# Moving q's stores and loads from SyncE's queue to GpSimd's, and splitting the first key segment ahead of q

## The chip, the cores and the metric

The kernel runs on one core of a Trainium2 chip. The metric is the time of one execution on the device in microseconds; the median of several executions is given. The trace is that of one profiled execution, whose times count from the start of its span.

## The reference

The program is one transformer layer with cross attention and a mixture of experts. What matters here is the attention in front:

```python
q = (layernorm(x) @ Wq + bq)        # x: 1024 x 128, 16 heads of 8
k = (ctx @ Wk + bk)                 # ctx: 6404 x 96
v = (ctx @ Wv + bv)
attn = softmax(clip(einsum('bhqd,bhkd->bhqk', q, k) * 8 ** -0.5, -1e4, 1e4))
x = x + einsum('bhqk,bhkd->bqhd', attn, v).reshape(1, 1024, 128) @ Wo + bo
x = x + ffn(layernorm(x))           # a main FFN and the best two of eight experts, gelu
```

All of it is computed in float32.

## The kernel before

**Stages.** First come the projections. TensorE transposes the context in 13 chunks of 512 keys (`ctx_transpose`), ScalarE copies each chunk to SBUF (`evac_ctxT`), TensorE projects it to keys (`project_k`) and ScalarE copies the result to `kT` (`evac_k`, semaphore `k_ready`). Between chunks 3 and 4 TensorE transposes the normalised x (`xnT`) and projects q, which ScalarE writes as `qT` (`q_ready`). VectorE does the layer norm ahead of that, copies `xnT` out of PSUM, and takes the largest absolute value of each chunk of `kT` (`range_k`), from which a bound on the scores is formed.

**Parts and round trips.** Scores are made with four-byte numbers of a rounded kind, so q and k are each split into a rounded part and the rest (`split_q`, `split_k`: one cast and one subtraction each). The parts go to DRAM and come back in another layout, in which the parts of the eight dimensions of one head stand on 32 partitions. For k this goes by ten segments of 640 keys: `split_k(s)` writes `kparts[:, s % 2]` (two buffers, so segment s waits until the store of segment s - 2 has landed), `store_k` stores it with two DMAs, `load_k` loads it to its place in `region_k`. For q it is once for all: `split_q` writes `qparts`, two stores go to `q_dram`, and then `load_q` loads each of four head groups with four DMAs of 32 partitions x 4 KB (each row of DRAM goes to two partitions) to `qst`. `qparts` lies in the first 2048 columns of `region_k`, in which the first key segments are to land later.

**Order.** All of these DMAs are on SyncE's queue (SP): the context and x, the two q stores, a wait for them, the loads of q's group 0, then the key segments' stores and loads in turn, then the loads of q's groups 1 to 3. GpSimd (POOL) makes constants, sets the row of ones in `region_ctxT` (after the last `xn`), sets the ones of `v9` and issues ten weight loads for later stages.

**Attention.** `score_tile(0)` waits for q's group 0 and key segment 0. Behind it on TensorE stand the projections of the first two chunks of v. Then follow 500 tiles of 3 x 512 scores: TensorE makes the scores (L1094), ScalarE the exponentials (L521), TensorE the products with v (L1179). Some score blocks go to VectorE instead, by a plan that is written out (`D_PLAN`) and starts at tile 37. The other v chunks, and the bounds, are spare jobs between the first tiles, and the splits of key segments 4 to 9 stand behind such v jobs. Segment s is first read some 6.7 s tiles into a pass (20 score blocks for each segment, three to a tile). All orders are fixed in the program: no engine chooses.

Of the kernel before, what the change touches and what calls it, by code (L numbers as in the profile page):

```python
# [22 lines left out]
NQ, C, CK, NK = 1024, 128, 96, 6404  # L23
# [10 lines left out]
BANK = 512  # L34
# [153 lines left out]
def build(nc, x, ctx, wq, bq, wk, bk, wv, bv, wo, bo, alpha, w_gate, b_gate, w1m, b1m, w2m, b2m,  # L188
# [4 lines left out]
    with ExitStack() as stack:  # L193
# [53 lines left out]
        q_abs = xn_flat  # L247
        att_tok = xn
        attT = xnT
        qparts = region_k[:, 0:PARTS * NQ].bitcast(F32R).rearrange("p (a n) -> p a n", a=PARTS)  # L250
        vtail = sb("vtail", [P, NG, P])
        qst = sb("qst", [P, NG, NQ], F32R)
        hid = [region[:, 0:CB * NQ].rearrange("p (c n) -> p c n", c=CB) for region in (region_kT[:, 2 * BANK:], region_ctxT)]
# [121 lines left out]
        def evac_k(act, c):  # L375
            a, b = c * BANK, min((c + 1) * BANK, NK)
            act.wait_ge(k_psum, c + 1)
            act.activation(kT[:, a:b], bank(3 + c % 3, P, b - a), ACT.Copy,
                           accum_out=ksum[:, c:c + 1]).then_inc(k_ready, 1)
# [8 lines left out]
        @block.sync  # L388
        def _(sp):

            rows = ctx[0, 0:FULL * P, :].rearrange("(p t) c -> p t c", t=FULL)
            for i, (t0, t1) in enumerate(zip(CTX_AT[:-1], CTX_AT[1:])):
                sp.dma_start(ctx_sb[:, t0:t1, :], rows[:, t0:t1, :]).then_inc(ctx_in[i], 16)
                if i == 0:
                    sp.dma_start(xres[:, :, :], x[0].rearrange("(t p) c -> p t c", p=P)).then_inc(x_in, 16)
            sp.dma_start(ctx_tail[:, :], ctx[0, FULL * P:NK, :]).then_inc(tail_in, 16)

            for b in range(PARTS):
                sp.wait_ge(qparts_ready, b + 1)
                sp.dma_start(q_dram[:, :, b, :], qparts[:, b, :].bitcast(F32)).then_inc(qparts_stored, 16)  # L400
            sp.wait_ge(qparts_stored, 16 * PARTS)
            load_q(sp, 0)
            for s in range(NSEG):
                store_k(sp, s)
                if s != 1:
                    load_k(sp, 0, max(s - 1, 0))
            load_k(sp, 0, NSEG - 1)
            load_k_tail(sp)
            for g in range(1, NG):
                load_q(sp, g)  # L410
            sp.wait_ge(flag_ready, 1)
            safe = sp.value_load(flag[0:1, 0:1], min_val=0, max_val=1)
            with sp.If(safe != 0):
                for g in range(1, NG):
                    for s in range(NSEG):
                        sp.wait_ge(scores_ready, tile_of_segment(NHALF * g - 1, s) + 1)
                        if spare_of_segment(g - 1, s):
                            sp.wait_ge(spare_psum, spare_of_segment(g - 1, s))
                        load_k(sp, g, s)
            with sp.Else():  # L420
                for s in range(NSEG):
                    sp.wait_ge(kst_in[s], 16)
                for g in range(NG):
                    sp.wait_ge(qst_in[g], 16 * GH)
                sp.wait_ge(ktail_in, 16 * NG)

            sp.wait_ge(topk_ready, 1)
            load_expert(sp, 0)
            for n, (t0, t1) in enumerate(OUT_TILES):
                sp.wait_ge(res_ready, n + 1)  # L430
                sp.dma_start(out[0, t0 * P:t1 * P, :].rearrange("(t p) c -> p t c", p=P), xn[:, t0:t1, :]).then_inc(out_stored, 16)
            sp.wait_ge(out_stored, 16 * len(OUT_TILES))


        @block.gpsimd
        def _(pool):
            pool.memset(ident[:, :], 0.0).then_inc(const_zero, 1)
            pool.memset(ones[:, :], 1.0).then_inc(const_ready, 1)
            pool.memset(hmask[:, :], 1.0).then_inc(const_zero, 1)
            pool.wait_ge(const_zero, 1)  # L440
            pool.affine_select(out=ident[:, :], in_=ident[:, :], compare_op=ALU.not_equal, fill=1.0, base=0,
                               pattern=[[-1, P]], channel_multiplier=1).then_inc(const_ready, 1)
            pool.wait_ge(const_zero, 2)

            pool.affine_select(out=hmask[:, :], in_=hmask[:, :], compare_op=ALU.is_ge, fill=0.0, base=0,
                               pattern=[[-D, H]], channel_multiplier=1).then_inc(const_zero, 1)
            pool.wait_ge(const_zero, 3)
            pool.affine_select(out=hmask[:, :], in_=hmask[:, :], compare_op=ALU.is_ge, fill=0.0, base=D - 1,
                               pattern=[[D, H]], channel_multiplier=-1).then_inc(const_ready, 1)
            pool.wait_ge(const_ready, 3)  # L450
            for dst, src in ((wv_sb[0:CK, :], wv), (wv_sb[CK:CK + 1, :], bv)):
                pool.dma_start(dst, src).then_inc(wv_in, 16)
            pool.memset(tailT[:, :], 0.0).then_inc(pads_ready, 1)
            pool.wait_ge(pads_ready, 1)
            pool.memset(ktail[:, :, :].bitcast(F32), 0.0).then_inc(pads_ready, 1)
            pool.wait_ge(pads_ready, 2)
            pool.wait_ge(xn_ready, QT)
            pool.memset(region_ctxT[CK:CK + 1, :], 1.0).then_inc(pads_ready, 1)
            pool.wait_ge(pads_ready, 3)
            pool.memset(v9[:, :, :, D:V9], 1.0).then_inc(vones_ready, 1)  # L460
            for dst, src in ((bsum[0:1, 0, :], bo), (wo_sb[:, :], wo), (mix[0:1, 3:4], alpha), (wg[:, :], w_gate), (bg[:, :], b_gate),
                             (w1m_sb[:, :], w1m), (w2m_sb[:, :, :], w2m.rearrange("(c p) d -> p c d", p=P)),
                             (b1rows[0:E * CB, :], b1e.rearrange("e (c p) -> (e c) p", p=P)),
                             (b1rows[E * CB:(E + 1) * CB, :], b1m.rearrange("a (c p) -> (a c) p", p=P)),
                             (b2rows[0:1, 0, :], b2m)):
                pool.dma_start(dst, src).then_inc(ffn_in, 16)

            pool.memset(vtail[:, :, :], 0.0).then_inc(vones_ready, 1)
            for j in range(GH):
                pool.wait_ge(vones_ready, 2 + j)  # L470
                pool.memset(vtail[QUAD * j:QUAD * j + TAIL, :, QUAD * j + D:QUAD * j + V9], 1.0).then_inc(vones_ready, 1)
            pool.wait_ge(vones_ready, 2 + GH)
            pool.memset(powers[:, :], -0.5).then_inc(powers_ready, 1)
            pool.wait_ge(powers_ready, 1)
            pool.memset(euler[:, :], math.e).then_inc(powers_ready, 1)
            pool.wait_ge(powers_ready, 2)
            for n in range(NHALF):
                pool.wait_ge(var_ready, 2 + n)
                r = slice(n * QT // 2, (n + 1) * QT // 2)
                pool.tensor_tensor(rstd[:, 3, r], rstd[:, 0, r], powers[:, 0:QT // 2], ALU.pow).then_inc(std_ready, 1)  # L480
            pool.wait_ge(msum_ready, 2)
            pool.tensor_tensor(gate[0:1, 2, :], euler[:, :], gate[0:1, 1, :], ALU.pow).then_inc(exp_gate, 1)
# [3 lines left out]
        def _(act):  # L486
# [6 lines left out]
            act.wait_ge(var_ready, 1)  # L493
            act.activation(rstd[:, 1, :], rstd[:, 0, :], ACT.Sqrt).then_inc(std_ready, 1)
            evac_k(act, 0)
            evac_ctxT(act, 1)
            evac_ctxT(act, 2)
            evac_k(act, 1)
# [9 lines left out]
            for c in range(4, KCH):  # L508
                if c + 1 < KCH:
                    evac_ctxT(act, c + 1)  # L510
                evac_k(act, c)
            act.wait_ge(table_step, 1)
            act.activation(scratch[:, :], ones[0:1, 0:1], ACT.Exp).then_inc(table_step, 1)

            def exponentials(tiles):

# [48 lines left out]
        def _(dve):  # L565
# [47 lines left out]
            scale_rows(range(QT))  # L613
            dve.wait_ge(wts_in, 48)
            v.tensor_scalar(bqs[:, :], bqc[:, :], QSCALE, None, ALU.mult).then_inc(bqs_ready, 1)
            for n in range(NHALF):
                dve.wait_ge(xnT_psum, n + 1)
                v.tensor_copy(xnT[:, n * BANK:(n + 1) * BANK], po[n][:, :]).then_inc(xnT_ready, 1)

            def range_k(c):  # L620

# [20 lines left out]
            def take_v(c, src):  # L642

                n = min(4, FULL + 1 - 4 * c)
                return v.tensor_copy(v9[:, 4 * c:4 * c + n, :, 0:D], src[:, 0:n * P].rearrange("p (t h d) -> p t h d", h=H, d=D))  # L645

            dve.wait_ge(wts_in, 48)
            link(v.tensor_scalar(kcol[:, 6:7], bkc[:, :], -1.0, None, ALU.mult))
            link(v.tensor_tensor(kcol[:, 1:2], kcol[:, 6:7], bkc[:, :], ALU.max))
            for c in range(KCH - 1):  # L650
                if c == 3:
                    split_q()
                    link(v.scalar_tensor_tensor(q_abs, qT[:, :], -1.0, qT[:, :], ALU.mult, ALU.max))
                range_k(c)
                if c in (2, 4, 7, 9):
                    split_k((2, 4, 7, 9).index(c), link)

            dve.wait_ge(ctxT_ready, KCH)
            dve.wait_ge(pads_ready, 3)
# [686 lines left out]
```

## Time and profile before

| | |
|---|---|
| median of 3 runs | 801.13 us (800.93 to 801.14) |
| the profiled execution's own time | 804.27 us |
| its span in the trace | 802.5 us |
| TensorE busy | 734.0 us, 91% of the span |
| ScalarE busy | 718.1 us, 89% |
| VectorE busy | 554.1 us, 69% |
| GpSimd busy | 21.0 us, 3% |

An engine's busy time counts neither waits nor DMA issues on its queue (shown as SPq, ACTq, POOLq). PEclk is the share of full clock that TensorE was granted: 1.0 is 2.4 GHz, 0.5 is 1.2 GHz.

### The profile page before, as it was taken

The numbers are of one execution on the slowest core, as the hardware profiler recorded it, in microseconds if no ns is written. First come the engines' busy times: TensorE is split into PE (matmuls) and PEld (weight loads), VectorE is DVE, ScalarE is ACT, GpSimd is POOL, SyncE is SP. The second block draws the span as 40 slices with busy tenths as digits, with TensorE's granted clock in tenths as the row PEclk, the third lists the DMA queues.
The fourth block names the chain that finished last, engine by engine and source line by source line (L and its number), as shares of the span: only waits on it lengthen the run. The fifth ranks groups of instructions, "written<-read, shape, count | busy, mean of one in ns | idle before, by whom it ended". The sixth has DMA issues, their size and how long they took to land.

```text
span 802.5 us, 13267 instructions
## 1 busy us (share of the span) xinstructions
PE 734.0 (91%) x5406; PEld 220.2 (27%) x5406; DVE 554.1 (69%) x776; ACT 718.1 (89%) x572; POOL 21.0 (3%) x36
## 2 busy tenths in 40 slices
PE   6469999999999998999999999999999999999798
PEld 3233322222222222222222222222222222222457
DVE  4344238879877978798868987897879782139320
ACT  4537899999999999999999999999999999999351
POOL 5200000000000000000000000000000000000000
PEclk9759999999999999999999999999999999999999
DMA  4455510011110000111110000111100000000010
GB/s 157 136 155 155 165 53 20 1 38 45 33 50 2 1 1 1 26 42 33 34 34 1 1 1 18 34 33 33 50 2 1 1 1 1 2 1 1 2 54 27
DMA packets 15323, 29.05 MB, mean 36 GB/s; under 512 B 2438, under 2 KB 5884, under 8 KB 15260
## 3 DMA queue, kind: packets, MB, share of 16 engines
q1 hardware_dynamic: 13562, 26.86, 10.9%
q8 instruction: 45, 0.74, 0.4%
q0 software_dynamic: 480, 0.66, 0.3%
q10 hardware_dynamic: 1218, 0.64, 0.3%
q14 instruction: 18, 0.15, 0.1%
HBM read 20.02 MB, written 8.13 MB: 35 GB/s over the span
## 4 chain that ended last, share of the span: by engine, by line
PE 57%; ACT 18%; issue 16%; DMA 4%; DVE 2%; SPq 1%; POOLq 0%; POOL 0%; ACTq 0%
PE po L1179 30%; PE ps L1094 17%; ACT region_ctx L521 14%; ACT probs_own L521 5%; PE po L1006 2%; PE ps L1274 2%; DMA k_dram<-kparts 1%; PE po L1284 1%; DMA region_ctx<-in_ctx 1%; DMA q_dram<-region_k 1%; PE po L1165 1%; PE po L1094 1%; PE po L1074 1%; DMA region_ctx<-in_w1e 1%; PE ps L1284 0%
## 5 line engine op out<-in xcount | busy, mean ns | idle before, releaser
L521 ACT ACTIVATE region_ctx<-ps 128x1536 f32<-128x1536 f32 x375 | 527.8, 1502 | 14.4 <-PE ps L1094 14.1
L1179 PE MATMUL po<-region_ctx,v 128*9 128x512 f32 x2238 | 391.5, 597 | 0.5 <-ACT region_ctx L521 0.5
L1094 PE MATMUL ps<-qst,region_k 32*128 32x512 f32 x1492 | 253.2, 497 | 52.2 <-ACT region_ctx L521 25.2
L1094 PEld LDWEIGHTS ps<-qst,region_k 32*128 32x128 f32 x1492 | 96.8, 182 | 424.4 <-ACT region_ctx L521 287.8
L521 ACT ACTIVATE probs_own<-ps 128x1536 f32<-128x1536 f32 x125 | 187.8, 1502 | 18.2 <-PE ps L1094 17.8
L1179 PE MATMUL po<-probs_own,v 128*9 128x512 f32 x746 | 192.9, 598 | 0.0
L802 DVE TENSOR_SCALAR region_kT<-po 128x512 f32<-128x512 f32 x108 | 74.1, 686 | 89.5 <-PE po L1094 89.5
L805 DVE SCALAR_TENSOR_TENSOR region_kT<-region_kT,po 128x512 f32<-128x512 f32 x108 | 73.4, 680 | 0.3
L841 DVE SCALAR_TENSOR_TENSOR dres<-region_kT,dres 128x1024 f32<-128x1024 f32 x54 | 66.1, 1225 | 1.7
L838 DVE SCALAR_TENSOR_TENSOR dres<-region_kT,dres 128x1024 f32<-128x1024 f32 x54 | 65.7, 1217 | 0.2
L830 DVE SCALAR_TENSOR_TENSOR dres<-region_kT 128x1024 f32<-128x1024 f32 x54 | 65.7, 1217 | 0.0
L832 DVE SCALAR_TENSOR_TENSOR region_kT<-region_kT 128x1024 f32<-128x1024 f32 x54 | 65.7, 1217 | 0.0
L835 DVE SCALAR_TENSOR_TENSOR dres<-dres,region_kT 128x1024 f32<-128x1024 f32 x54 | 65.5, 1214 | 0.0
L1179 PEld LDWEIGHTS po<-region_ctx,v 128*9 128x9 f32 x2238 | 42.3, 88 | 69.9 <-issue 66.2
L1094 PE MATMUL po<-qst,region_k 32*128 32x512 f32 x108 | 51.4, 476 | 0.0
L821 DVE TENSOR_SCALAR region_kT<-region_kT 128x1024 uint32<-128x1024 uint32 x54 | 36.9, 683 | 0.0
L645 DVE COPY v<-po 128x512 f32<-128x512 f32 (+1 forms) x13 | 8.8, 680 | 33.9 <-PE po L1006 33.9
L1179 PE MATMUL po<-dres,vd 128*9 128x512 f32 x216 | 28.2, 595 | 0.0
L1179 PEld LDWEIGHTS po<-probs_own,v 128*9 128x9 f32 x746 | 19.6, 88 | 23.0 <-issue 22.6
L480 POOL TENSOR_TENSOR rstd<-rstd,powers 128x4 f32<-128x4 f32 x2 | 2.1, 1027 | 728.5 <-DVE rstd L592 728.5
L1094 PEld LDWEIGHTS po<-qst,region_k 32*128 32x128 f32 x108 | 19.6, 181 | 1.3 <-issue 1.3
L639 DVE CAST kparts<-region_kT 128x640 fp32r<-128x640 f32 (+1 forms) x10 | 5.1, 512 | 18.5 <-DMA k_dram<-kparts 18.5
(201 smaller groups left out, 324.8 us busy)
## 6 DMA issues: line engine op xcount, KB each, us to landing
region_k<-k_dram SPq DMA_DIRECT2D x40, 320.0 KB, 3.3
k_dram<-kparts SPq DMA_DIRECT2D x18, 320.0 KB, 3.7
qst<-q_dram SPq DMA_DIRECT2D x16, 128.0 KB
region_ctx<-in_ctx SPq DMA_DIRECT2D x2, 624.0 KB, 9.9
q_dram<-region_k SPq DMA_DIRECT2D x2, 512.0 KB, 4.5
k_dram<-kparts SPq DMA_DIRECT2D x2, 322.0 KB, 3.3
region_ctx<-in_ctx SPq DMA_DIRECT2D x1, 576.0 KB, 8.3
xres<-in_x SPq DMA_DIRECT2D x1, 512.0 KB, 4.4
```

The source lines that it names most:

```text
L521: act.activation(probs_of(t), ps[t % NSB][:, :], ACT.Exp, scale=ESCALE).then_inc(exp_ready, 1)
L802: d_count(("u", c), v.tensor_scalar(du[:, i % 2, part], src, MAGIC, None, ALU.add))
L805: v.scalar_tensor_tensor(df[:, i % 2, part], du[:, i % 2, part], MAGIC, src, ALU.subtract, ALU.subtract).then_inc(spare_taken, 1)
L821: d_count(("e", i), v.tensor_scalar(u.bitcast(U32), u.bitcast(U32), 23, None, ALU.logical_shift_left))
L830: d_count(("q1", i), v.scalar_tensor_tensor(res, f, A1, f, ALU.add, ALU.mult))
L832: d_count(("q2", i), v.scalar_tensor_tensor(q, f, A2, f, ALU.add, ALU.mult))
L835: d_count(("p1", i), v.scalar_tensor_tensor(res, res, B1, u, ALU.add, ALU.mult))
L838: d_count(("p2", i), v.scalar_tensor_tensor(res, q, B2, res, ALU.add, ALU.mult))
L841: v.scalar_tensor_tensor(res, f, R0, res, ALU.subtract, ALU.mult).then_inc(d_ready, 1)
L1006: last = mm(dst[:, (t % 4) * P:(t % 4 + 1) * P], lhsT, wv_sb[:, :], start=True, stop=True)
L1094: return mm(dst, kst[r, kt * P:(kt + 1) * P], qst[r, g, queries], start=True, stop=True)
L1179: last = mm(dst[QUAD * j:QUAD * j + V9, :], w, src, start=first, stop=last_one, skip_group_check=True)
```

## The change

The two q stores, the wait for them and all q loads move from SyncE's queue to GpSimd's, behind the ten weight loads; the memset of the ones in `v9` moves behind the loads of q's group 0. `qparts` moves from `region_k` to `dres`, a buffer that the VectorE exponentials use from tile 37 on. On VectorE `split_k(0)` moves ahead of the `xnT` copies, `range_k(3)` ahead of `split_q`, and `q_abs` and `split_k(1)` change places around chunk 4. On ScalarE the load of the exponential's table (with an activation of one element) moves from behind the last `evac_k` to behind the first.

```diff
-        qparts = region_k[:, 0:PARTS * NQ].bitcast(F32R).rearrange("p (a n) -> p a n", a=PARTS)
+        qparts = dres[:, 0, 0:PARTS * NQ].bitcast(F32R).rearrange("p (a n) -> p a n", a=PARTS)
...
             sp.dma_start(ctx_tail[:, :], ctx[0, FULL * P:NK, :]).then_inc(tail_in, 16)
 
-            for b in range(PARTS):
-                sp.wait_ge(qparts_ready, b + 1)
-                sp.dma_start(q_dram[:, :, b, :], qparts[:, b, :].bitcast(F32)).then_inc(qparts_stored, 16)
-            sp.wait_ge(qparts_stored, 16 * PARTS)
-            load_q(sp, 0)
             for s in range(NSEG):
                 store_k(sp, s)
                 if s != 1:
                     load_k(sp, 0, max(s - 1, 0))
             load_k(sp, 0, NSEG - 1)
             load_k_tail(sp)
-            for g in range(1, NG):
-                load_q(sp, g)
...
             pool.memset(region_ctxT[CK:CK + 1, :], 1.0).then_inc(pads_ready, 1)
-            pool.wait_ge(pads_ready, 3)
-            pool.memset(v9[:, :, :, D:V9], 1.0).then_inc(vones_ready, 1)
             for dst, src in ((bsum[0:1, 0, :], bo), (wo_sb[:, :], wo), (mix[0:1, 3:4], alpha), (wg[:, :], w_gate), (bg[:, :], b_gate),
...
+            for b in range(PARTS):
+                pool.wait_ge(qparts_ready, b + 1)
+                pool.dma_start(q_dram[:, :, b, :], qparts[:, b, :].bitcast(F32)).then_inc(qparts_stored, 16)
+            pool.wait_ge(qparts_stored, 16 * PARTS)
+            load_q(pool, 0)
+            pool.wait_ge(pads_ready, 3)
+            pool.memset(v9[:, :, :, D:V9], 1.0).then_inc(vones_ready, 1)
+            for g in range(1, NG):
+                load_q(pool, g)
             pool.memset(vtail[:, :, :], 0.0).then_inc(vones_ready, 1)
...
             evac_k(act, 0)
+            act.wait_ge(table_step, 1)
+            act.activation(scratch[:, :], ones[0:1, 0:1], ACT.Exp).then_inc(table_step, 1)
             evac_ctxT(act, 1)
...
-            act.wait_ge(table_step, 1)
-            act.activation(scratch[:, :], ones[0:1, 0:1], ACT.Exp).then_inc(table_step, 1)
...
-            for n in range(NHALF):
-                dve.wait_ge(xnT_psum, n + 1)
-                v.tensor_copy(xnT[:, n * BANK:(n + 1) * BANK], po[n][:, :]).then_inc(xnT_ready, 1)
...
+            dve.wait_ge(k_ready, 2)
+            split_k(0, link)
+            for n in range(NHALF):
+                dve.wait_ge(xnT_psum, n + 1)
+                v.tensor_copy(xnT[:, n * BANK:(n + 1) * BANK], po[n][:, :]).then_inc(xnT_ready, 1)
...
             for c in range(KCH - 1):
+                range_k(c)
                 if c == 3:
                     split_q()
+                if c == 5:
                     link(v.scalar_tensor_tensor(q_abs, qT[:, :], -1.0, qT[:, :], ALU.mult, ALU.max))
-                range_k(c)
-                if c in (2, 4, 7, 9):
-                    split_k((2, 4, 7, 9).index(c), link)
+                if c in (4, 7, 9):
+                    split_k(1 + (4, 7, 9).index(c), link)
```

## Rows read from the trace of the kernel before

**Rows 1.** Windows: stretch, length, busy us (instructions) of PE, PEld, DVE, ACT, POOL, clock, DMA share, GB/s.
```profile
30.00:35.00 5.00, 0.08 (x1) 0.00 (x0) 0.00 (x0) 2.23 (x6) 0.00 (x0) 0.68 0.48 156
35.00:40.00 5.00, 0.00 (x0) 0.00 (x0) 0.00 (x0) 0.00 (x0) 0.00 (x0) 0.50 0.13 52
...
62.00:64.00 2.00, 2.00 (x14) 0.42 (x8) 0.68 (x1) 1.06 (x1) 0.00 (x0) 0.88 0.88 247
...
200.00:300.00 100.00, 94.59 (x736) 22.82 (x733) 82.72 (x101) 99.97 (x75) 0.00 (x0) 1.00 0.06 18
```

**Rows 2.** The chain that ended last, in order of time: start us, us, what.
```profile
21.07 1.24 DVE region_k L631
...
22.32 6.07 DMA q_dram<-region_k
...
31.79 11.29 DMA k_dram<-kparts
...
43.09 3.55 DMA region_k<-k_dram
...
46.78 0.79 PE ps L1094 x2
...
59.01 1.83 PE po L1179 x8
...
72.24 0.98 PE po L1179 x8
```

**Rows 3.** Timeline of SP's queue, 0 to 130 us.
```profile
28.41 2.68 SPq L367 DMA_DIRECT2D qst<-q_dram  x4
...
95.09 17.21 SPq L367 DMA_DIRECT2D qst<-q_dram  x12
```

**Rows 4.** Timeline of POOL (GpSimd), 0 to 100 us.
```profile
11.66 5.45 POOL L458 MEMSET region_ctxT<- 1x6432 f32 x1 [7.37 <-DVE xn L597]
17.18 1.58 POOL L460 MEMSET v<- 128x816 f32 x1
18.59 0.49 POOL L466 DMA_DIRECT2D bsum<-in_bo  x1
...
24.51 0.55 POOL L468 MEMSET vtail<- 128x512 f32 x1
```

**Rows 5.** DMA issues: queue, count, KB each, us from issue to landing.
```profile
region_k<-k_dram SPq DMA_DIRECT2D x40, 320.0 KB, 3.3
k_dram<-kparts SPq DMA_DIRECT2D x18, 320.0 KB, 3.7
...
w2m_sb<-in_w2m POOLq DMA_DIRECT2D x1, 256.0 KB, 5.6
...
wo_sb<-in_wo POOLq DMA_DIRECT2D x1, 64.0 KB, 2.1
```

**Rows 6.** Timeline of DVE (VectorE), 0 to 100 us.
```profile
15.72 1.29 DVE L618 COPY xnT<-po 128x512 f32<-128x512 f32 x2 [4.12 <-PE po L1020]
...
17.30 1.87 DVE L624 TENSOR_REDUCE kmax<-region_kT 128x1 f32<-128x512 f32 x3
19.08 0.48 DVE L639 CAST kparts<-region_kT 128x640 fp32r<-128x640 f32 x1
19.60 0.82 DVE L640 TENSOR_TENSOR kparts<-region_kT,kparts 128x640 fp32r<-128x640 f32 x1
```

**Rows 7.** Timeline of ACT (ScalarE), 0 to 100 us.
```profile
10.36 0.59 ACT L373 ACTIVATE region_ctxT<-ps 96x512 f32<-96x512 f32 x1 [1.29 <-PE ps L983]
...
13.61 0.19 ACT L378 ACTIVATION_READ_ACCUMULATOR region_kT<-ps 128x1 f32 x1
...
19.76 0.19 ACT L506 ACTIVATION_READ_ACCUMULATOR qT<-po,bqs 128x1 f32 x1
...
30.76 1.28 ACT L513 ACT_TABLE_LOAD   x1
```

## The prediction

> **What bounds the kernel now.** I read the windows first. From 200 to 300 us ScalarE is busy 99.97 of 100 us at the full clock [rows 1], one stretch of many alike. The order of the tiles is fixed, so this long middle only moves with its start: what the change touches lies ahead of the first score. There the windows from 30 to 40 us show a hole. TensorE does 0.08 us of work from 30 to 35 us and none from 35 to 40 us, VectorE none in either [rows 1].
>
> The chain in order of time says what fills the hole [rows 2]. The rest of q is formed from 21.07 us (1.24 us). The q store takes 6.07 us, to 28.39. SP then issues four q loads, 2.68 us [rows 3], and the store of key segment 0 lands 11.29 us after 31.79 us, at 43.08. Its load takes 3.55 us, and at 46.78 us comes the first score [rows 2]. So the key path, ready early, waits behind q on SP's queue.
>
> The 11.29 us need a second look. The same kind of store takes 3.7 us in the median [rows 5]. From 35 to 40 us the DMA engines are busy at a share of 0.13, 52 GB/s [rows 1]: 0.13 x 16 is two engines. What is in flight then is the four q loads of 128 KB and what stands behind them. 512 KB at 52 GB/s is 10.1 us, so the q loads, issued by 31.09 us, end at about 41.2 us. I read this as q loads confined to two engines, with the key store's share on these two standing behind them. Then q itself is not there before 41.2 us, and key segment 0 only 5.5 us later. Mending the order alone brings 5.5 us at most; more hangs on how fast q loads on GpSimd's queue.
>
> **The key path after the change.** `split_k(0)` needs two key chunks; the second is written by 13.80 us [rows 7], and VectorE has waited since 11.6 us (15.72 less 4.12 us of waiting [rows 6]). The split takes 1.34 us, from 19.08 to 20.42 in its old place [rows 6], so it ends at 15.2 us. The `xnT` copies start at 15.72 us when TensorE is done [rows 6]: 0.5 us of cover, cost nothing; without it, q and all behind it would be late by what is missing. SP has nothing else then. It issues two stores (0.6 us each, as the load issues of rows 3), the last lands 3.7 us later, at 19.6, and the load 3.3 us after that [rows 5]: segment 0 at 23 us, against 46.6. `qparts` in `dres` is what lets this load go ahead of the q store; `dres` is first used from tile 37 on.
>
> Later segments: the new order of VectorE gives `split_q` its start at 19.95 us, when `qT` is complete [rows 7] (one more range, 0.62 us, lies ahead of it, but the split is gone from there), and q is split by 21.9 us instead of 22.31. `split_k(1)` ends at about 24 us, `split_k(2)` at 28.5 and `split_k(3)` at 31 (ranges of 0.62 us, splits of 1.3 us, `q_abs` 1.2 us in line), with no wait for the stores of segment 0, which cost VectorE 15 us before. Segment 1 then lands at about 33 us and is read first at tile 6. Cost nothing. What hides it is the time until the first score; segment 2 has another six or seven tiles. Segments 4 to 9 are split behind v jobs and move with TensorE.
>
> **The table load.** It takes 1.28 us, and its activation 0.2 us [rows 7]. In its old place, 30.76 us, ScalarE was idle behind it, so nothing is gained. In the new one ScalarE had waited 1.29 us until 10.36 us [rows 7], so `evac_ctxT(1)` comes 0.2 us late. TensorE is then still busy transposing chunk 2 and reads the copy after that: 0.1 us at most, on a path with 0.4 us of cover or more. Should the copies need another table load, that is 1.28 us more on this path (and once more before the first exponential, in the hole). No row shows copies under the exponential's table: I take 0, with 1.3 us as the other bound.
>
> **The q path, on GpSimd's queue.** This now sets the start. GpSimd's memset of the row of ones ends at 17.11 us and its ten weight issues took from 18.59 to 24.51 us, 5.92 us [rows 4]. They now follow the row of ones directly (the `v9` memset, 17.18, moved): 17.2 to 23.1 us. q has been ready since 21.9, so GpSimd's issues, not VectorE, are last. Two store issues of 0.6 us: the second starts at 23.7. For its landing I take 5.6 us, that of w2m on this queue; q's own second store took 6.07 us [rows 2, 5]. q stored: 29.3 us, about 1 us later than before (28.39). Four load issues of 0.6 us: the last starts at 31.1 us.
>
> The trace has no broadcast load on this queue, so the loads are bounded from both sides. Fast: the four spread over all engines; then the last lands like the 64 KB load wo, 2.1 us [rows 5], with 0.3 us for its data at eight times 52 GB/s: 33.5 us. Slow: all four on the same two engines, 10.1 us from about 31: 41 us, and up to 46 if key segments 1 and 2 take turns on these two (their data is as much again). Between: each load on two engines, but not the same two. One load's 128 KB at 52 GB/s is 2.5 us: 31.1 + 2.1 + 2.5 = 35.7 us. I take this one. That SP's loads used two engines shows how one such load is cut; that the pairs differ on this queue no row shows.
>
> The Trainium skill, DMA: Bandwidth & Descriptors, section Why a DMA increments its semaphore by 16 and not by 1, states that a load is cut over as many engines as divide the slowest dimension of both sides (here 2), on SP's queue always the lowest-numbered ones, on GpSimd's consecutive ones from a cursor that moves on. By that rule the sum is the one between (35.7 us); by the row of 35 to 40 us alone it would be the slow one. The trace agrees for SP (share 0.13).
>
> Behind the loads of group 0 GpSimd sets the ones of `v9`, 1.58 us: done by 35 us, first used some 7 us after the first score. The twelve loads of groups 1 to 3 took SP 17.21 us to issue [rows 3]; at worst the same here, to 52 us. Behind them wait only `vtail`'s memsets, first needed after the last v job (114 us before). Taking the twelve from SP at 95 us frees nothing that waits, since group 1's key segments are loaded tens of us later. Their 1.5 MB pass beside key segments 1 to 3, which have tiles of slack.
>
> **The sum.** The first score moves from 46.78 to 35.8 us (q at 35.7, 0.1 to the start): 11.0 us. TensorE's clock: the mean of 0.68 from 30 to 35 us means full clock for 1.8 us, so it fell to 1.2 GHz at 31.8, 1.8 us after TensorE went idle, and it rose again at 62.5 (0.88 over 62 to 64) [rows 1], 15.7 us after the restart. In that stretch eight value products take 1.83 us against 0.98 [rows 2]. Nothing changes before 31.8 us, so the clock falls again; I take 15.7 us at 1.2 GHz again, moved as a whole. A rise some 3 us early or late is worth up to 1.5 us. Everything from 47 us on moves by 11.0: span 802.5 - 11.0 = 791.5, this execution's own time 804.27 - 11.0 = 793.3, and the median, 801.13, goes to **790.1 us**.
>
> **The rivals.**
> - **All engines** share each q load: q at 33.5, first score 33.6, gain 13.2: 787.9 us. For it: other loads on this queue land in 2.1 us. Against it: SP's share of 0.13 for this very shape.
> - **The same two engines** on GpSimd's queue too: q at 41 to 46 us: gain 5.8 to 0.7; 795.3 to 800.4 us, likeliest 796. For it: the 0.13; against it: nothing in the rows.
> - **The clock** stays up or returns sooner, as the hole shrinks from 16.7 to 5.7 us: half speed costs at most 15.7 x (1 - 0.98/1.83) = 7.3 us, so down to 782.8 us. Against it: it fell within 1.8 us of idleness.
> - **Nothing moves** within 0.2% (1.6 us, about what a measurement can tell here): the slow end above at 46 us.
> - **Slower**: GpSimd can't write q's descriptors while VectorE runs its fast casts and copies, which fill 20 to 31 us. Every one of the two stores and four loads is on the path, so it breaks even at 11.0/6 = 1.8 us added to each, three times the 0.6 us of an issue; at 2.5 us added to each it gives 805.1 us (790.1 + 15). Against it: the ten weight issues ran from 18.59 to 24.51, beside such work, at 0.59 us each [rows 4], and in the new order three casts of 0.48 us [rows 6] lie in the way, at most 1.5 us: 791.6.
>
> The Trainium skill, SBUF — State Buffer, section SBUF: two separate sides, warns of this lock, and the section after it gives 620 ns alone against 3,100 ns beside a copy. By those figures six DMAs would cost 15 us, an estimate from that page, and the kernel would be slower; the weight issues of 0.59 us speak against it.
>
> **How the numbers follow.** Forecast 52%, own range 787.5 to 793. All engines 15%. The same two engines 20%, of which 2 within 0.2%. The clock 6%. The lock on a scale that costs the whole gain 4%. Another cause within 0.2% 3%. The range of 785.5 to 796.5 leaves out 8 of the two engines' 20, 4 of the clock's 6 and the last two cases: 19%. Faster by over 0.2%: 52 + 15 + 18 + 6 = 91%; within it 2 + 3 = 5%; slower 4%.
>
> **What will show it.** In the trace after: the store of segment 0 issued near 15.3 us and its load landed by 23; GpSimd's q stores near 23.1, its loads from 29.3; the first score at 35.8 with its wait ended by q's load, not the keys'; a DMA share well over 0.13 while q loads; half clock from 31.8 to about 51.5; and from there the same tiles 11 us earlier. I am wrong if the first score waits past 40 us, if GpSimd's issues stretch past 1 us, if `xnT` is copied after 16 us, or if later tiles give back what the start gained.

## The result: 0.3% faster, where 1.4% was forecast

| | before | after |
|---|---|---|
| median of 20 runs | 802.44 us (800.12 to 804.85) | 800.22 us (797.46 to 801.97) |
| the profiled execution's own time | 804.27 us | 800.87 us |
| its span | 802.5 us | 798.8 us |
| first score (start) | 46.78 us | 42.77 us |
| from there to the end of the span | 755.7 us | 756.0 us |

The ratio of the means of the two is 0.9967 (95% interval 0.9956 to 0.9977): faster, by 2.2 us in the medians where 11.0 were forecast, and outside the stated range of 785.5 to 796.5 us. The last two rows of the table, both from the profiled execution, say where the question lies: behind the first score next to nothing changed, and ahead of it 4.0 us were gained instead of 11.0.

**The chain of the changed kernel**, in order of time (start us, us, what), answers to [rows 2]:

```profile
14.07 3.54 DVE kparts L636
...
17.64 0.82 DVE kparts L637
18.46 1.20 DVE xnT L648 x2
...
19.95 2.46 DVE kmax L621 x4
22.41 0.61 DVE dres L626
23.05 1.24 DVE dres L628
24.28 0.29 issue
24.57 5.41 DMA q_dram<-dres
29.99 0.28 issue
30.27 2.07 POOL qst L367 x3
32.34 10.38 DMA qst<-q_dram
...
42.77 0.80 PE ps L1097 x3
```

The key store is gone from it, as meant, and so is the load of key segment 0. The chain ends with q. Two pieces are far longer than forecast: the cast of `split_k(0)` with 3.54 us (0.48 in [rows 6]) and the last q load, which lands 10.38 us after its issue (4.6 forecast).

**Windows of the changed kernel** (columns as in [rows 1]):

```profile
30.00:35.00 5.00, 2.11 (x8) 0.92 (x6) 4.46 (x11) 2.19 (x8) 4.69 (x7) 1.00 0.73 194
35.00:40.00 5.00, 0.00 (x0) 0.00 (x0) 0.00 (x0) 0.00 (x0) 5.00 (x9) 0.54 0.97 300
...
55.00:60.00 5.00, 5.00 (x21) 0.79 (x21) 2.48 (x4) 1.45 (x1) 0.00 (x0) 0.57 0.36 99
```

From 35 to 40 us all compute engines but GpSimd are idle as before, but the DMA engines are not: a share of 0.97 and 300 GB/s, where [rows 1] have 0.13 and 52. Something else moves now while q is awaited. The queue's timelines name it.

**Timelines of the changed kernel, SP's queue and GpSimd** (answering to [rows 3] and [rows 4]):

```profile
18.49 1.27 SPq L344 DMA_DIRECT2D k_dram<-kparts  x2
24.32 0.57 SPq L354 DMA_DIRECT2D region_k<-k_dram  x1
26.16 5.46 SPq L344 DMA_DIRECT2D k_dram<-kparts  x4
31.70 0.84 SPq L354 DMA_DIRECT2D region_k<-k_dram  x1
33.09 1.40 SPq L344 DMA_DIRECT2D k_dram<-kparts  x2
37.96 0.56 SPq L354 DMA_DIRECT2D region_k<-k_dram  x1
```

```profile
11.79 5.46 POOL L451 MEMSET region_ctxT<- 1x6432 f32 x1 [7.46 <-DVE xn L597]
...
24.57 0.82 POOL L461 DMA_DIRECT2D q_dram<-dres  x1 [0.69 <-DVE dres L628]
30.27 2.65 POOL L367 DMA_DIRECT2D qst<-q_dram  x4 [4.88 <-DMA q_dram<-dres]
32.96 1.56 POOL L465 MEMSET v<- 128x816 f32 x1
34.37 6.97 POOL L367 DMA_DIRECT2D qst<-q_dram  x12
```

SP, freed from q, issues the stores of key segments 1 to 3 and the loads of 1 and 2 from 26 to 38.5 us, just when q's loads run, and none of these is needed before tile 6. GpSimd's memset of one row lies exactly over the place (14.07 us) to which `split_k(0)` was moved.

### The profile page after: what moved, and what is told of

Read it like the earlier page. It is cut to its first block, busy times and chain, and to the rows that moved or that the text cites. A ratio compares the mean times of both kernels' runs of the same rounds, so it can differ in the third digit from the quotient of the medians.

```text
span 798.8 us, 13267 instructions
## 1 busy us (share of the span) xinstructions
PE 734.8 (92%) x5406; PEld 220.1 (28%) x5406; DVE 557.1 (70%) x776; ACT 717.9 (90%) x572; POOL 31.8 (4%) x54
## 3 DMA queue, kind: packets, MB, share of 16 engines
q0 software_dynamic: 5120, 3.83, 1.8%
## 4 chain that ended last, share of the span: by engine, by line
PE 57%; ACT 19%; issue 17%; DVE 3%; DMA 3%; POOL 0%; POOLq 0%; SPq 0%; ACTq 0%
PE po L1182 31%; PE ps L1097 17%; ACT region_ctx L521 14%; ACT probs_own L521 5%; PE po L1009 2%; PE ps L1277 2%; PE po L1287 1%; DMA qst<-q_dram 1%; PE po L1168 1%; DMA q_dram<-dres 1%; PE po L1097 1%; DMA xres<-in_x 1%; PE po L1077 1%; DMA region_ctx<-in_w1e 1%; PE ps L1287 0%
## 5 line engine op out<-in xcount | busy, mean ns | idle before, releaser
L1009 PE MATMUL po<-wv_sb,region_ctxT 97*128 97x128 f32 x100 | 17.0, 323 | 0.0
```

Of the source, the lines that this page charges most:

```text
L1009: last = mm(dst[:, (t % 4) * P:(t % 4 + 1) * P], lhsT, wv_sb[:, :], start=True, stop=True)
```

## The experiments

All are built on the changed kernel, except the eleventh, which is built on the kernel before. "First score" is the start of the first score matmul in the profiled execution. The ratio is that of the means, against the kernel before in runs of the same chip. A first score is that of one execution and carries that execution's own scatter: the `xnT` copies start at 15.72 us in the kernel before and at 13.99 in the eleventh kernel, which is the same program up to there. Differences of under 2 us between two first scores are therefore read together with the pieces of the chain, or with the medians.

| | first score | span | median | ratio (95% interval) |
|---|---|---|---|---|
| split of segment 0 behind `xnT` | 42.02 | 796.8 | 799.24 | 0.9963 (0.9945 to 0.9982) |
| groups 1 to 3 late | 42.62 | 806.3 | 799.55 | 0.9966 (0.9955 to 0.9977) |
| keys late | 38.35 | 794.3 | 795.59 | 0.9921 (0.9904 to 0.9937) |
| q on SP's queue | 43.31 | 797.9 | 800.24 | 0.9981 (0.9968 to 0.9993) |
| pieces, on SP's queue | 36.31 | 793.9 | 793.48 | 0.9876 (0.9847 to 0.9904) |
| pieces, on GpSimd's queue | 39.63 | 794.5 | 796.40 | 0.9922 (0.9895 to 0.9950) |
| row of ones early | 38.16 | 793.2 | 795.20 | 0.9900 (0.9870 to 0.9929) |
| pieces and keys late | 36.13 | 790.9 | 792.72 | 0.9881 (0.9848 to 0.9913) |
| all three, two queues | 30.35 | 784.5 | 786.38 | 0.9811 (0.9791 to 0.9830) |
| the same, v ahead | 32.46 | 787.1 | 787.34 | 0.9815 (0.9796 to 0.9834) |
| kernel before, pieces alone | 37.79 | 792.9 | 794.89 | 0.9913 (0.9893 to 0.9932) |
| table late | 42.63 | 797.2 | 800.30 | 0.9970 (0.9956 to 0.9983) |

### What holds the cast: `split_k(0)` behind the copies

```diff
-            dve.wait_ge(k_ready, 2)
-            split_k(0, link)
             for n in range(NHALF):
                 dve.wait_ge(xnT_psum, n + 1)
                 v.tensor_copy(xnT[:, n * BANK:(n + 1) * BANK], po[n][:, :]).then_inc(xnT_ready, 1)
+            dve.wait_ge(k_ready, 2)
+            split_k(0, link)
```

> The changed kernel with split_k(0) put back behind the xnT copies, nothing else. In the changed kernel its cast took 3.53 us instead of 0.48, beside GpSimd's memset of the row of ones (11.79 to 17.25 us). If GpSimd's memset holds up VectorE's cast: behind the xnT copies the cast starts at 17.0 us and takes about 0.5 to 0.7, the copies start near 15.9 instead of 18.46, qT is complete near 20.0 instead of 22.0, the last q part near 22.2 instead of 24.28. q's second store is then issued when the weight issues end (23.1 to 23.7) instead of 24.57, so the first score moves by about 0.9 us (42.8 to about 41.9), the median by -0.5 to -1.5 us against the changed kernel. If instead the cast is long for another reason (its buffer, its source just written by ScalarE): it takes about 3.5 us in the new place too and nothing moves.

VectorE in the changed kernel, and then in this one (timelines):

```profile
14.07 3.53 DVE L636 CAST kparts<-region_kT 128x640 fp32r<-128x640 f32 x1 [2.34 <-ACT region_kT L378]
```

```profile
16.02 1.29 DVE L646 COPY xnT<-po 128x512 f32<-128x512 f32 x2 [4.27 <-PE po L1023]
17.23 0.48 DVE L636 CAST kparts<-region_kT 128x640 fp32r<-128x640 f32 x1
```

The cast takes 0.48 us again. In this kernel GpSimd's memset runs from 11.82 to 17.28 us, and the cast starts at its end; in the changed kernel the cast starts at 14.07, inside the memset (to 17.25), and ends at 17.60, 0.35 us after it. Two more kernels with the same order bear it out: the cast starts at 14.57 and takes 2.85 us (pieces and keys late), or at 13.40 and takes 4.16 us (table late), and ends 0.36 us after the end of the memset each time. The copies out of PSUM at 16.02 run beside the memset unhindered. The first score moved by 0.75 us (0.9 expected): less than the 2.4 us by which the copies moved, since q then waits for GpSimd's weight issues, as forecast. The medians of the two kernels come from different runs and stay within their scatter.

### Are the loads behind it in the way: groups 1 to 3 late

```diff
+            pool.wait_ge(scores_ready, 1)
             for g in range(1, NG):
                 load_q(pool, g)
```

> The changed kernel with GpSimd's twelve loads of q's groups 1 to 3 held until the first score tile is made. If they are what makes the loads of group 0 land 8 to 10 us after their issue: group 0 lands within 5 us of its last issue, first score near 37 instead of 42.8 us, median 4 to 6 us lower. If the loads of group 0 are slow by themselves or through the key segments: the first score stays at 42 to 43 us and the median within 1 us of the changed kernel.

First score at 42.62 us, the last load of group 0 landing 10.30 us after its issue: the twelve loads behind it are not the cause. (The long span of this profiled execution goes with a mean granted clock of 0.938, against 0.985 in the changed kernel's; the median, 799.55, is within 1 us of the changed kernel's 800.22.)

### Are the keys in the way: segments 2 and on late

```diff
             for s in range(NSEG):
+                if s == 2:
+                    sp.wait_ge(qst_in[0], 16 * GH)
                 store_k(sp, s)
```

> The changed kernel with SyncE's stores of key segments 2 and on (and the loads behind them) held until q's group 0 has landed. If the key segments' traffic slows q's loads: group 0 lands 2 to 5 us sooner, first score at 38 to 41 us. If q's loads are slow by themselves or through groups 1 to 3: first score at 42 to 43 us. Either way the key segments 1 and 2 come later, near 47 us, still ahead of their tiles.

The chain of this kernel:

```profile
32.25 6.06 DMA qst<-q_dram
...
38.35 0.80 PE ps L1099 x2
```

The same loads, issued at the same time, land 4.3 us sooner. The key segments' traffic, which the change itself had moved into this stretch, costs 4.3 of the 5.8 us that the term was short. The median is 4.6 us below that of the changed kernel (3.7 us by the two ratios).

Windows of this kernel while the loads run, and for comparison one of the changed kernel:

```profile
32.00:34.00 2.00, 0.14 (x1) 0.00 (x0) 1.97 (x4) 0.80 (x4) 1.96 (x3) 1.00 0.53 58
32.00:38.00 6.00, 0.14 (x1) 0.00 (x0) 2.46 (x8) 0.80 (x4) 5.96 (x10) 0.80 0.61 107
```

```profile
32.00:38.00 6.00, 0.11 (x1) 0.00 (x0) 2.54 (x8) 0.77 (x4) 5.96 (x10) 0.78 0.93 266
```

The DMA engines are not free here either: from 34.29 us the loads of groups 1 to 3 are issued behind those of group 0. By the issues, the first window holds only group 0's loads. Its share of 0.53 is some eight of the 16 engines, which fits the forecast's reading of two engines for each of four loads and not the same two, but they move only 58 GB/s together, where two engines moved 52 for SP [rows 1]. By this reading, which no experiment tests, the spread was forecast rightly and the rate of each engine was not; why the rate is lower on this queue, no run shows.

### What the queue is worth: q on SP's queue, behind segment 0

```diff
             for s in range(NSEG):
                 store_k(sp, s)
                 if s != 1:
                     load_k(sp, 0, max(s - 1, 0))
+                if s == 0:
+                    for b in range(PARTS):
+                        sp.wait_ge(qparts_ready, b + 1)
+                        sp.dma_start(q_dram[:, :, b, :], qparts[:, b, :].bitcast(F32)).then_inc(qparts_stored, 16)
+                    sp.wait_ge(qparts_stored, 16 * PARTS)
+                    load_q(sp, 0)
```

(The corresponding lines are taken from GpSimd's queue; groups 1 to 3 stand at the end of SP's. GpSimd's memset of the ones of `v9` so comes right behind the weight loads.)

> The changed kernel with q's stores and loads back on SyncE's queue, behind the store and load of key segment 0 (groups 1 to 3 at the end of that queue, as in the kernel before). It has the new buffer, the new order of splits and the early table load, and only not the queue. If all of the gain came from the order (key segment 0 ahead of q): q is stored near 28.5 to 29.5, its loads take 10 us at two engines' rate after their issue, first score near 42, the same as the changed kernel or up to 1 us better. If GpSimd's queue brings a gain of its own: first score at 44 us or later.

The chain of this kernel:

```profile
25.20 5.01 DMA q_dram<-dres
...
32.31 10.96 DMA qst<-q_dram
...
43.31 0.80 PE ps L1098 x2
```

Its window from 30 to 35 us has a DMA share of 0.16. So the loads take 11 us on SP's queue with the keys behind them, and 10.4 us on GpSimd's with the keys beside them: moving them brought 0.5 us of first score at most, and the medians, 800.24 and 800.22, show none of it. Of the change's 4.0 us the order, the buffer and the rest of the edit bring 3.5 or all. Only with the keys held does GpSimd's queue show that it handles these loads better, 6.06 us.

### The shape of the loads

```diff
-            for j in range(GH):
-                rows = q_dram[GH * g + j, :, :, :].rearrange("d r n -> (d r) n")
-                sp.dma_start(qst[QUAD * j:QUAD * (j + 1), g, :].bitcast(F32),
-                             rows.unsqueeze(0).broadcast_to([PARTS, PARTS * D, NQ])).then_inc(qst_in[g], 16)
+            for e in range(PARTS):
+                for j in range(GH):
+                    rows = q_dram[GH * g + j, :, :, :].rearrange("d r n -> (d r) n")
+                    r0 = QUAD * j + PARTS * D * e
+                    sp.dma_start(qst[r0:r0 + PARTS * D, g, :].bitcast(F32), rows).then_inc(qst_in[g], 16)
```

(The waits for these loads count twice as many landings.)

> The kernel with q on SyncE's queue behind key segment 0 (e4_q_on_sync), with each q load of 32 partitions cut into two of 16 partitions x 4 KB that read the same 16 rows: 8 loads for group 0, the same bytes. If a load's shape (a broadcast over two outer halves) is what confines it to two engines: a plain load of 16 rows spreads, the last of 8 issues is at about 30.2 + 7 x 0.65 = 34.8 us and lands 2.5 to 3 us later, first score near 37.5 instead of 43.3 us, median 4 to 6 us lower than with e4_q_on_sync. If the 10 us come from elsewhere (key stores on the same queue, DRAM): the first score stays at 42 us or later, or grows by the 2.6 us of the four more issues.

> The kernel before, with only the shape of q's loads changed: each in two of 16 partitions, all on SyncE's queue in the old order, 8 issues for group 0. If the 10 us of the q loads, and of the key store behind them, come from the shape: the store of segment 0 lands about 4 us after its issue instead of 11.3, segment 0 is loaded near 40.5, first score near 41 instead of 46.8 us, median 5 to 6 us below the kernel before, more than the whole change under study brings. If the queue is what matters: first score at 46 us or later, and nothing gained.

The chain with the pieces on SP's queue behind segment 0, and then that of the kernel before with nothing but the pieces:

```profile
33.29 0.42 SPq L369
33.75 2.52 DMA qst<-q_dram
36.31 0.80 PE ps L1099 x3
```

```profile
30.01 0.64 SPq L344
30.69 3.43 DMA k_dram<-kparts
34.13 3.52 DMA region_k<-k_dram
...
37.79 0.80 PE ps L1095 x3
```

The last of the eight lands 2.52 us after its issue, where the last of four took 10.96 us. The issues got cheaper too: 0.46 us from one to the next instead of about 0.7, so that eight take 3.56 us. In the kernel before, the store of segment 0 now takes 3.43 us instead of the 11.29 of [rows 2]. So it was the shape of q's loads that held this store, as the prediction read that row; that they stood on two engines is the reading of the share of 0.13. Part of the sooner first score there (37.79; 41 expected) is that this execution's q store was issued at 21.90 and landed by 26.4, in 4.49 us instead of 6.07. One shape, nothing moved, gives 0.9913: two and a half times the gain of the whole change.

The Trainium skill, DMA: Bandwidth & Descriptors, section Why a DMA increments its semaphore by 16 and not by 1, gives the rule that a load is cut by the largest number up to 16 that divides the slowest dimension on both sides: 2 for the broadcast, 16 for the pieces. These runs agree on SP's queue, with 10.96 against 2.52 us.

> The changed kernel with the same pieces on GpSimd's queue. If the shape confines q's loads there too: first score near 38.5 us (issues from 30.3 to 35.5, landing 3 us later, key traffic beside it), median 3 to 4 us below the changed kernel. If GpSimd's queue spreads them already and the key segments' traffic is the whole cost: first score unchanged at 42 to 44 us.

> The changed kernel with the pieces on GpSimd's queue (as e6_pieces_pool) and the key segments from 2 on held until q's group 0 has landed (as e3_keys_late). If shape and key traffic are two separate costs: first score at 37 to 37.5 us (issues end at 35.5, landing 2 us), earlier than either alone (38.35 with the keys held alone). If they are one and the same cost, it equals the better of the two alone, or is a little later through four more issues.

On GpSimd's queue the pieces land 6.19 us after the last issue with the keys beside them (first score 39.63), and with the keys late:

```profile
33.48 2.61 DMA qst<-q_dram
36.13 0.80 PE ps L1100 x2
```

So both costs exist there as well. With the keys held, shape is worth 6.06 - 2.61 = 3.5 us of landing, though four more issues give back 1.2. With the pieces, holding the keys is worth 3.6 us. The rows of the profile's page show one more trait of the broadcast on this queue: GpSimd's queue moved 5,120 packets in the changed kernel and 1,792 with the pieces, for the same 3.8 MB.

### The row of ones early

```diff
-            pool.wait_ge(xn_ready, QT)
             pool.memset(region_ctxT[CK:CK + 1, :], 1.0).then_inc(pads_ready, 1)
```

> The changed kernel without the wait for xn ahead of GpSimd's memset of the row of ones, so that it runs from about 4.4 to 9.9 us instead of 11.8 to 17.3. If that memset is what held VectorE's cast: split_k(0)'s cast takes 0.5 us at 14.1, the xnT copies start at 15.9, the last q part is ready at 22.2 instead of 24.28, and GpSimd has issued its weights by about 16 us and waits for q. q stored near 27.5 to 28.5 instead of 29.99, first score 1.5 to 2.5 us earlier (40.3 to 41.3). VectorE's normalisation of x at 9.5 us may be held for up to 0.4 us. If the cast was long for another reason, it stays at 3.5 us.

VectorE's timeline:

```profile
8.37 1.51 DVE L589 TENSOR_SCALAR rstd<-mv 128x8 f32<-128x8 f32 x1
...
15.57 0.49 DVE L635 CAST kparts<-region_kT 128x640 fp32r<-128x640 f32 x1 [2.34 <-ACT region_kT L378]
```

The cast is free, but another instruction now meets the memset (4.39 to 9.84 us): this one takes 1.51 us, 0.17 in the kernel before, and ends at the memset's end. All behind it is 1.5 us late, and the last q part is ready at 24.7, no sooner. Yet the first score comes at 38.16: the q store takes 3.25 us instead of 5.41, and the last q load lands 7.80 us after its issue instead of 10.38. The expectation (40.3 to 41.3) named the wrong source of the gain and half its size. Two things are out of the q store's way here: the weight loads, all issued by 15.35 us (23.11 in the changed kernel), and the load of key segment 0, issued at 21.08 instead of 24.32. Which of the two counts, and why the q loads are faster with about the same key traffic, these runs do not tell.

### All three mended, and v ahead of the first score

The memset of the row of ones goes ahead of the loads of `wv` and of the two other memsets of that stage, q's loads are pieces, and for group 0 one half of them has a semaphore of its own on SP's queue, for which TensorE waits too:

```diff
             pool.wait_ge(const_ready, 3)
+            pool.memset(region_ctxT[CK:CK + 1, :], 1.0).then_inc(pads_ready, 1)
             for dst, src in ((wv_sb[0:CK, :], wv), (wv_sb[CK:CK + 1, :], bv)):
...
-            load_q(pool, 0)
+            load_q(pool, 0, [0])
...
+                if s == 0:
+                    sp.wait_ge(qparts_stored, 16 * PARTS)
+                    load_q(sp, 0, [1], qst_sp)
```

> The changed kernel with three things mended. GpSimd's memset of the row of ones stands right behind its constants (about 2.0 to 7.5 us), where VectorE waits for x. q's stores stay on GpSimd's queue. Each q load is two loads of 16 partitions; for group 0 one half of them goes on GpSimd's queue and the other on SyncE's, whose key segments from 1 on stand behind them. If lock, shape and key traffic are the three costs, each is now gone: cast of segment 0 0.5 us at 14, q's parts ready at 22.2, q stored near 26 to 27, loads issued by 29, landed by 31.5: first score at 31 to 33 us, some 4 us ahead of the best so far (36.1), median 786 to 790 us. If the first score comes no sooner than 35 us, one of the three is not understood.

The chain:

```profile
13.00 0.73 DVE kparts L640
13.75 0.83 DVE kparts L641
14.57 1.20 DVE xnT L652 x2
...
20.68 4.35 DMA q_dram<-dres
...
26.76 3.55 DMA qst<-q_dram
30.35 0.79 PE ps L1103 x2
```

First score at 30.35 us, 16.4 us ahead of the kernel before; the median is 16.3 us lower (802.70 to 786.38). TensorE waited 1.97 us for q. Part of this first score is the execution's own: the `xnT` copies start at 14.49 us, where 15.9 was expected with a free cast. The median is what says that this version beats both kernels, and it lies in the expected range.

```diff
-            score_tile(0)
             pe.wait_ge(q_ready, NHALF)
             project_v(0, po[0]).then_inc(v_psum, 1)
             project_v(1, po[1]).then_inc(v_psum, 1)
+            score_tile(0)
```

> As e9_halves_two_queues, and TensorE projects the first two chunks of v ahead of the first score tile. If TensorE's work behind the first score (3.7 us at 1.2 GHz) is on the path and fits into the hole, the second score tile follows the first at once, and TensorE is idle for so short a time that the clock may stay up: 3 to 9 us less than e9_halves_two_queues. If the exponentials (ScalarE) set the pace right after the start, under 1 us less.

Nothing gained: the medians are 787.34 and 786.38. The chain, and a line of TensorE's timeline:

```profile
28.51 4.90 DMA k_dram<-kparts
33.42 0.51 DVE kparts L640
...
34.70 1.27 DVE kmax L625 x2
...
36.25 0.59 DVE v L646
...
37.98 0.60 DVE v L646
```

```profile
38.72 1.04 PE L1188 MATMUL po<-probs_own,v 128*9 128x512 f32 x3 [2.19 <-DVE v L646]
```

VectorE is to copy v out of PSUM, but stands at `split_k(3)`, which waits for the store of segment 1. The value products wait 2.19 us for these copies and start at 38.72 us, against 38.02 without this edit. Half of the expectation came true: the second score tile follows the first at once, and the granted clock falls only at 36.2 us (0.61 from 36 to 37), where it fell at 30.2 without the edit (0.60 from 30 to 31). But the work then stands before the wait on VectorE, and the medians gain nothing by it. The two executions can't be compared closely, since the last q part is ready at 22.61 us here and at 20.40 there, ahead of anything that the edit touches.

### The table load

> The changed kernel with the exponential's table loaded where it was before. Its load lies in the hole there. If the early load is worth nothing, and costs at most the 0.3 us by which it delays evac_ctxT(1): first score 0 to 0.3 us earlier than 42.77, median within 1 us of the changed kernel. If copies under the other table are slower or faster, the ScalarE rows from 10 to 33 us show it.

The edit puts the two lines of the table load back behind the last `evac_k`. The medians are 800.30 and 800.22: worth nothing, as forecast. The first scores, 42.63 us against 42.77, would not show it alone: in this execution TensorE's granted clock was 0.50 from 20 to 22 us, the last q part was ready at 25.62 instead of 24.28, and the q store (4.68 us) and the last q load (9.95 us) made up for it. The copies from 96x512 take 0.59 us under either table.

## Why the prediction was wrong, step by step

- **What bounds the kernel**: right. The pieces in the kernel before show that the key store stood behind q's loads, and that their shape was the reason (11.29 to 3.43 us); the share of 0.13 stands for the two engines.
- **The middle moves as a whole**: right, 755.7 and 756.0 us from first score to end. Over all kernels the gain in the median lies within 2.2 us of the gain in the first score: 16.4 us of the one give 16.3 of the other, 8.4 (keys late) give 6.3, 4.0 give 2.2 in the medians and 3.4 in the profiled executions. Part of the last gap is that the profiled execution of the kernel before took 804.27 us, 1.8 above its median.
- **The clock**: right in kind. The mean of 0.54 from 35 to 40 us puts the fall at 35.4 us and the 0.57 from 55 to 60 the rise at 59.3, 16.5 us after the restart (15.7 assumed). The fall was forecast at 31.8, since "nothing changes before 31.8 us"; but with `xnT` late TensorE's projections ended at 32.1 us instead of 30.1.
- **"0.5 us of cover, cost nothing"** for `split_k(0)`: wrong. The cast met GpSimd's memset, whose row stood in [rows 4], and took 3.53 us. I had the lock among the rivals, but only in one direction, VectorE holding up GpSimd; that one did not come, with 0.57 and 0.82 us for the issues of q's stores and 0.69 for those of its loads. The held cast cost the copies 2.7 us, the last q part 1.97 us (24.28 against 22.31 before, where 21.9 was forecast), and the first score 0.75 us by the two executions (q's second store is issued 0.99 us sooner with the split behind).
- **The keys: "Cost nothing"**: this is the step that failed. I priced the keys' earlier traffic by who waits for it, and nobody does. I did not price what it takes from q: the q loads land 4.3 us later for it (10.38 against 6.06 us, shown). The bound of 46 us named this collision only for q on the same two engines. For the forecast case it was left at nothing.
- **The landing of q's loads**, 2.1 + 2.5 = 4.6 us: 6.06 us with the keys held, so 1.5 us short in itself, and 10.38 in place. The 2.5 us in it took each engine at the rate of SP's; the window of the keys-late kernel (share 0.53, 58 GB/s) has more engines at a lower rate.
- **The store** of q: 5.41 us against 5.6 taken, right, though it was issued at 24.57 us instead of 23.7, behind the late q part. The loads' issues took 0.69 us each, with 0.28 us ahead of the first.

The sum of the miss: the last load is issued at 32.34 instead of 31.1 us (1.2), lands 10.38 instead of 4.6 us later (5.8), together the 7.0 us between 42.77 and 35.8. The rival nearest to what came is the one of the same two engines, by its time of q (41 to 46 us), though its cause was another: not two engines again, but other traffic beside it.

## What to carry to other kernels

When an edit lets transfers start earlier, price them twice: by who waits for them, and by what is in flight at their new time. A transfer that nobody needed yet was better held here until the one that everybody waited for had landed: 4.3 us with the broadcast loads, 3.6 with the pieces. Read the DMA share of a hole before mending its order: 0.13 pointed to loads on two engines, and its shape was worth more than all of the reordering. Before moving an instruction of VectorE, look at what GpSimd does at the new place.

## What was not expected of the hardware

- A GpSimd memset of one partition by 6,432 elements (5.46 us) holds VectorE's cast of 128 x 640 to just behind its end (3.53 instead of 0.48 us), and in another place a `tensor_scalar` of 128 x 8 (1.51 instead of 0.17 us). The memset of the ones of `v9` (1.58 us) does it too: in the kernel before with the pieces, the cast starts 0.14 us behind its start, takes 1.79 us and ends 0.35 us behind its end. The statistics of x (1.64 us) and the copies out of PSUM (1.29 us for two) ran beside it at their usual time. The Trainium skill, SBUF — State Buffer, section SBUF: two separate sides, says that whichever of the two starts first keeps the shared port for its whole instruction; these rows agree.
- Four loads of 128 KB that each read 16 rows twice took 10.96 us on SP's queue from the last issue to landing; eight of 64 KB for the same bytes take 3.56 us to issue and 2.52 us to land.
- The same broadcast on GpSimd's queue took 6.06 us with the key segments held (107 GB/s in all from 32 to 38 us) and 10.38 us with them (266 GB/s). How the queues share an engine there, no run shows.
